# A language-model layer on one core: GpSimd's running sums move behind its scaling, its residual sum moves to the group's second sequence, and VectorE looks up the largest logits' places half an octet later

## The chip, the cores and the metric

The kernel runs on one core of one Trainium2 chip. The metric is the device time of one execution in microseconds (us); lower is better. The engines are called PE (TensorE matmul), PEld (TensorE weight load), DVE (VectorE), ACT (ScalarE), POOL (GpSimd) and SP (SyncE).

## The reference

128 sequences of 128 tokens go through an embedding, one attention layer and one mixture-of-experts layer. Cut to what matters:

```
h = concat(pos, nest, seg embeddings) @ W                    # 128 wide
h = h + attention(layernorm(h))                              # 8 heads of 64, causal softmax
x = layernorm(h)
logits = x @ router_w.T + router_b                           # 8 experts
val, idx = top_k(logits, 2); w = softmax(val)
out = h + sum_k w[k] * expert[idx[k]](x)                     # 128 -> 2*256 -> silu gate -> 128
```

## The kernel before

The kernel has two stages. The attention stage (from about 20 us to 870 us) takes the 128 sequences one after the other, and also computes, for each token, its two experts and the row that it gets in an expert-sorted table in DRAM; POOL scatters the normed tokens there with indirect DMAs. The expert stage (from about 870 us to the end) reads that table in blocks of 256 rows, and runs the experts.

In the attention stage four sequences form a group (`GB`), two groups an octet (`OB` = 8). `octet_steps` writes out by hand the order of the steps of one octet; every engine walks the same list and picks the kinds that concern it, in that order. Octets 0 and 1 are written out, octets 2 to 14 are a loop, and the last octet has an order of its own (`final_steps`, with `FINAL`). I call the stretch of one sequence a slot, number it n = 0 to 3 within its group, and call four slots a half. In each slot PE does, for the sequence k of the slot: query and key of the next group (L1209 to L1211), the scores of k (L1302, with the causal mask at L1310), then for the sequence before it, k-1, the transposes of its probabilities, first half at L1321 and second half at L1326, then one value product (L1286), the output projection (L1351) of k-2, a filler (embedding or route matmuls), and the mix (L1338) of k-1.

The probabilities come from ACT (eight exponentials with sums, L737). They are scaled by one over their sums in two halves: the first by POOL (step `scale0`, L557, which waits for DVE's reciprocals at L873 and L874), the second by DVE (step `scale1`, L946). PE's L1321 waits for the first, its L1326 for the second. scale1 of k is done in the slot after k; scale0 of k in the slot of k.

Beside this, spread over the four slots of a half:

- DVE, slot 3: `route_ranks` (copy of PE's counts, L1016), `onehot` (L883), the reciprocals, `route_logits` (L1033, L1048), `route_top` (L984 MAX8, then L990, pairs of MATCH_VALUE_LOAD and FIND_INDEX8 for each sequence, which give the places of the largest logits), `route_weight` (L1008, L1010, L1012). Slot 2: `route_choose` (L994, L997, L1003) for the group of one half earlier, reciprocals, `route_norm` (L962, L968), the low part of the transposed input (L919).
- POOL, slot 3: `route_ranks`, seven small operations that keep the running sums of rows given out per expert (L592 four times, L594, L598, L599), then `scale0`, then `residual` (L573, the bias added to h of the next group, 128x544; then L578), then two indirect DMAs of the scatter (L609). Slot 0: scale0, `rstd` (L525, L527), two DMAs. Slot 1: scale0, a small addition (L542), two DMAs. Slot 2: scale0, `route_rstd` (L533, L535), two DMAs.

The residual sum waits on a semaphore count of `scaled1`: before it can start, DVE must have scaled the last sequence of the current group, which it does at the beginning of the next slot. POOL's queue is in order, so the two DMAs behind the residual sum wait too. The first consumers of the residual are PE's and DVE's projection of the next group (L957) and the `embed_add` in slot 0 of the next half. In octet 1 POOL also has a step `w1_lo` (L561) at the end of each slot. In the last octet POOL does no scale0 (DVE does both halves, L939 and L946), and DVE's `route_apply` (L1040) waits for the scatter of two groups before.

Of the kernel before, what the change touches and what calls it, by code (L numbers as in the profile page):

```python
# [23 lines left out]
GB = 4  # L24
# [16 lines left out]
LEAD = 64  # L41
# [6 lines left out]
def octet_steps(octets_done):  # L48

    steps = []  # L50

    def late(*step):
        if step[1] + octets_done * (OB if step[0] in PER_SEQUENCE else 2) >= 0:
            steps.append(step)

    for k in range(OB):
        half, n = k // GB, k % GB
        steps.append(("query", half + 1, n))
        steps.append(("key", half + 1, n))
        steps.append(("scores", k))  # L60
        late("scale1", k - 1)
        steps.append(("max", k))
        if octets_done == 0 and k == 0:
            steps.extend(("value", 0, n) for n in range(GB))
            steps.append(("onehot", 2))
        late("probsT", k - 1)
        steps.append(("value", half + 1, n))
        late("project", k - 2)
        steps.append(("exp", k, 0))
        if n == 0:  # L70
            steps += [("embed", half + 2), ("embed_add", half + 2)]
        elif n == 1:
            steps += [("embed_r", half + 2), ("norm", half + 2)]
        elif n == 2:
            steps.append(("normT", half + 2))
            late("route_choose", half - 2)
        elif n == 3:
            late("route_ranks", half - 2)
            steps.append(("onehot", half + 3))
        steps += [("exp", k, 1), ("scale0", k)]  # L80
        late("mix", k - 1)
        if n == 0:
            steps += [("stats", half + 2), ("rstd", half + 2)]
            late("route_rows", half - 3)
        elif n == 1:
            late("route_apply", half - 2)
        elif n == 2:
            late("route_norm", half - 1)
            late("route_rstd", half - 1)
            steps.append(("xlo", half + 2))  # L90
        elif n == 3:
            late("route_logits", half - 1)
            late("route_top", half - 1)
            late("route_weight", half - 2)
            steps.append(("residual", half + 1))
        late("scatter", half - 3, 2 * n, 2 * n + 2)
        if octets_done == 0:
            steps.extend(("pad", n) for n in ((2 * k, 2 * k + 1) if k < GB else (GB + k,)))
            steps.append(("w1_hi", k))
        if octets_done == 1:  # L100
            steps.append(("w1_lo", k))
    return steps


FINAL = (
    ((("route_rows", -3), ("route_apply", -2), ("route_choose", -2)), (("scatter", -3, 0, 4),)),
    ((("route_ranks", -2), ("route_weight", -2)), (("scatter", -3, 4, 8),)),
    ((("route_rows", -2), ("route_norm", -1)), (("route_rstd", -1), ("scatter", -2, 0, 4))),
    ((("route_scale", -1), ("route_top", -1)), (("residual", 1), ("scatter", -2, 4, 8))),
    ((("route_choose", -1), ("route_ranks", -1), ("route_weight", -1)), ()),  # L110
    ((("route_rows", -1), ("route_norm", 0)), (("route_rstd", 0), ("scatter", -1, 0, 4))),
    ((("route_scale", 0), ("route_top", 0), ("route_choose", 0)), (("scatter", -1, 4, 8),)),
    ((("route_ranks", 0), ("route_weight", 0)), ()),
)


def final_steps():

    steps = []
    for k in range(OB):  # L120
        if k < GB:
            steps += [("query", 1, k), ("key", 1, k)]
        steps += [("scores", k), ("scale1", k - 1), ("max", k), ("probsT", k - 1)]
        if k < GB:
            steps.append(("value", 1, k))
        steps += [("project", k - 2), ("exp", k, 0), ("exp", k, 1), ("mix", k - 1)]
        steps += [*FINAL[k][0], ("scale0", k), *FINAL[k][1]]
    steps += [("scale1", OB - 1), ("route_rows", 0), ("scatter", 0, 0, 4)]
    steps += [("probsT", OB - 1), ("project", OB - 2), ("mix", OB - 1), ("project", OB - 1)]
    steps += [(w, 1) for w in ("route_norm", "route_rstd", "route_logits", "route_top", "route_choose", "route_ranks",  # L130
                               "route_apply", "route_weight", "route_rows")]
    return steps + [("scatter", 1, 0, 4), ("scatter", 0, 4, 8), ("scatter", 1, 4, 8)]

# [11 lines left out]
def build(nc, a, out, codes_dram, xs, spare, nseq):  # L145
# [12 lines left out]
    with ctx:  # L158
        def sb(name, shape, dt=F32):
            return ctx.enter_context(nc.sbuf_tensor(name, shape, dt))  # L160
# [78 lines left out]
        residual = [sb(f"residual{i}", [S, GB, D2]) for i in range(2)]  # L239
# [227 lines left out]
        def _(pool):  # L467
            own = [0]

            def link(ins):  # L470
                own[0] += 1
                ins.then_inc(p_own, 1)
                pool.wait_ge(p_own, own[0])
# [44 lines left out]
            def step(o, st, opening=False):  # L518
                kind, i = st[0], st[1]
                if kind == "rstd":  # L520
                    G = 2 * o + i
# [6 lines left out]
                elif kind == "route_rstd":  # L528
                    G = 2 * o + i
# [6 lines left out]
                elif kind in ("route_scale", "route_apply"):  # L536
                    G = 2 * o + i
# [25 lines left out]
                elif kind == "residual":  # L563
                    G = 2 * o + i
# [4 lines left out]

                    pool.wait_ge(h2_ready, LEAD + GB * (G - 1))  # L570
                    if not opening:
                        pool.wait_ge(scaled1, LEAD + GB * G)
                    pool.tensor_tensor(residual[i % 2][:], h[i % 2][:], bias_o[:].unsqueeze(1).broadcast_to([S, GB, D2]),  # L573
                                       ALU.add).then_inc(residual_ready, 1)
                    pool.wait_ge(rstd_ready, LEAD + G + 1)
# [3 lines left out]
                elif kind == "vsplit":  # L579
                    pool.wait_ge(tab_copied, 6)  # L580
                    link(pool.tensor_tensor(v_full_t, v_full_t, v_rest, ALU.subtract))
                    link(pool.tensor_copy(v_rest, v_full_t))
                    link(pool.tensor_scalar(v_part, v_rest, part_mask[:, 2:3], None, ALU.mult))
                    link(pool.tensor_tensor(v_full_t, v_full_t, v_part, ALU.subtract))
                    pool.tensor_copy(v_table[:], v_full_t).then_inc(s_vtable, 1)
                elif kind == "route_ranks":
                    G = 2 * o + i
                    pool.wait_ge(ranks_ready, LEAD + G + 1)
                    pool.wait_ge(filled_next, LEAD + G)
                    carry_wait(pool)  # L590
                    for j in range(GB):
                        pool.tensor_tensor(filled[:, j + 1], filled[:, j], ranks[:, 1, :, j], ALU.add).then_inc(filled_step, 1)  # L592
                        pool.wait_ge(filled_step, LEAD + GB * G + j + 1)
                    pool.tensor_tensor(rows_f[:], ranks[:, 0], filled[:, 0:GB].rearrange("p j k e -> p k j e"), ALU.add).then_inc(rows_c, 1)  # L594
                    pool.wait_ge(rows_c, LEAD + G + 1)
                    pool.wait_ge(rows_b, LEAD + G)
                    carry_wait(pool)
                    pool.tensor_tensor(rows_2[:], rows_f[:], chosen[:], ALU.mult).then_inc(rows_a, 1)  # L598
                    pool.tensor_copy(filled[:, 0], filled[:, GB]).then_inc(filled_next, 1)  # L599
                elif kind == "scatter":  # L600
                    G, par = 2 * o + i, i % 2
                    pool.wait_ge(row_ready, LEAD + G + 1)
                    pool.wait_ge(weight1_ready, LEAD + G + 1)
                    pool.wait_ge(token_ready, LEAD + G + 1)
                    pool.wait_ge(normed2_ready, LEAD + G + 1)
                    pool.wait_ge(h2_stored[par], LEAD + 16 * (o + (i - par) // 2 + 1))
                    carry_wait(pool)
                    for k, j in [divmod(n, GB) for n in range(st[2], st[3])]:
                        pool.indirect_dma_start((xs[0], xs_parts)[k], bass.IndirectOffsetOnAxis(ap=row[par][:, k, j:j + 1].bitcast(U32), axis=0),  # L609
                                                normed2[par][:, j, 0:(ROW, PART)[k]], None).then_inc(scattered[par][k], 16)  # L610
# [15 lines left out]
                for st in octet_steps(2):  # L626
                    step(o, st)
            steps = final_steps()
            n = steps.index(("route_ranks", 1)) + 1
            for st in steps[:n]:  # L630
                if st[0] != "scale0":
                    step(octets - 1, st)
# [173 lines left out]
        def _(dve):  # L806
# [69 lines left out]
            def step(o, st, opening=False, final=False):  # L876
                kind, i = st[0], st[1]
                G, b, par = 2 * o + i, OB * o + i, i % 2
# [100 lines left out]
                elif kind == "route_top":  # L979
# [3 lines left out]
                    for j in range(GB):  # L983
                        ins = V.max(top[:, j], logits[:, j])  # L984
                    ins.then_inc(top_ready, 1)
                    dve.wait_ge(top_ready, LEAD + G + 1)
                    dve.wait_ge(top_no_ready, LEAD + G)
                    carry_wait(dve)
# [487 lines left out]
```

## Time and profile before

| | |
|---|---|
| median of 3 runs | 1311.32 us (1310.25 to 1314.24) |
| the profiled execution | 1309.72 us, of which its span in the trace is 1307.9 us |
| PE busy / DVE / ACT / POOL, whole span | 92% / 81% / 73% / 66% |
| one half (four sequences) in the loop | about 24.9 us |

The span is what lies between the first and the last instruction; 1.8 us of the profiled execution lie around it. In a timeline row the columns are start (us from the span's start), duration, engine, line, operation, out<-in with shapes, count, and in brackets how long the engine was idle before it and who released it. Matmuls of one line are merged in one row, and their starts say more than their durations: where PE has no wait, the distance from one start to the next is the same in each half.

### The profile page before, as it was taken

How to read it: one execution, taken by the hardware profiler on the slowest of the kernel's cores; microseconds unless marked ns; L12 is line 12 of the kernel's file. 1: busy time of each engine (PE TensorE's matmuls, PEld its weight loads, DVE VectorE, ACT ScalarE, POOL GpSimd, SP SyncE). 2: the span in 40 equal slices, each digit the busy share in tenths (PEclk: the TensorE clock that was granted, in tenths of full speed). 3: DMA queues.
4: the chain of work that ended last, by engine and by line, in shares of the span. 5: the costliest groups of instructions: out<-in, count | busy, mean ns of one | idle time of the engine just before them, and what ended most of it. 6: DMA issues, size and time to landing. Idle time of an engine off the chain costs nothing. (4 is left out here: it accounts for less than half of the span.)

```text
span 1307.9 us, 47296 instructions
## 1 busy us (share of the span) xinstructions
PE 1196.9 (92%) x13772; PEld 1027.0 (79%) x13773; DVE 1053.9 (81%) x3980; ACT 955.4 (73%) x3352; POOL 865.8 (66%) x1207
## 2 busy tenths in 40 slices
PE   6889899999999999999999999728999997999995
PEld 4577787787877877788788787617999997899995
DVE  6568988888888888888888887747888885888885
ACT  2788899999999899989999998714555553555552
POOL 6335767767767766776776776765677774667775
PEclk8899999999999999999999999959999998999998
DMA  6141111111111111111111111238999997999994
GB/s 186 66 175 47 46 46 38 57 43 39 53 47 39 47 53 39 39 57 41 38 55 43 39 57 44 68 107 275 318 348 349 329 339 230 313 337 345 346 343 164
DMA packets 95043, 184.65 MB, mean 141 GB/s; under 512 B 18236, under 2 KB 42500, under 8 KB 94852
## 3 DMA queue, kind: packets, MB, share of 16 engines
q1 hardware_dynamic: 54404, 63.45, 15.9%
q10 hardware_dynamic: 20736, 75.80, 15.4%
q0 software_dynamic: 19840, 44.62, 9.6%
q8 instruction: 32, 0.52, 0.2%
q14 instruction: 31, 0.25, 0.1%
HBM read 46.45 MB, written 53.18 MB: 76 GB/s over the span
## 5 line engine op out<-in xcount | busy, mean ns | idle before, releaser
L737 ACT ACTIVATE probs<-ps,neg_max 128x128 f32<-128x128 f32 (+1 forms) x1024 | 336.7, 368 | 1.3 <-DVE neg_max L924 1.3
L609 POOL DMA_INDIRECT xs<-normed,row x256 | 260.8, 1019 | 70.5 <-issue 66.7
L737 ACT ACTIVATION_READ_ACCUMULATOR probs<-ps,neg_max 128x1 f32 x1024 | 240.1, 236 | 0.0
L1209 PE MATMUL ps<-xT_hi,w_now 128*128 128x256 f32 x576 | 178.8, 310 | 18.6 <-DVE xT_lo L1094 9.3
L693 ACT ACTIVATE masked<-ps,w_now 128x256 f32<-128x256 f32 x288 | 121.0, 471 | 74.2 <-PE ps L1211 69.2
L557 POOL TENSOR_TENSOR probs<-probs,inv_sums 128x384 f32<-128x384 f32 x120 | 100.1, 834 | 103.9 <-DVE inv_sums L874 103.2
L1211 PE MATMUL ps<-xT_hi,w_now 128*128 128x256 f32 x576 | 163.4, 284 | 0.0
L1210 PE MATMUL ps<-xT_lo,w_now 128*128 128x256 f32 x576 | 163.3, 284 | 0.0
L1123 DVE SCALAR_TENSOR_TENSOR probsT<-ps,w_now,masked 128x256 f32<-128x256 f32 x288 | 126.1, 479 | 43.7 <-PE ps L1211 29.9
L1391 PE MATMUL ps<-w,probsT 128*128 x1152 | 153.4, 276 | 3.0 <-DVE probsT L1123 3.0
L746 ACT ACTIVATE probsT<-ps,rstd_now 128x512 f32<-128x512 f32 x128 | 88.4, 690 | 83.7 <-PE ps L1321 75.0
L1391 PEld LDWEIGHTS ps<-w,probsT 128*128 128x128 f32 x1152 | 142.1, 193 | 3.6 <-issue 3.6
L1351 PEld LDWEIGHTS ps<-w_o,mixedT 128*128 128x128 f32 x1024 | 140.1, 193 | 6.1 <-issue 1.1
L1351 PE MATMUL ps<-w_o,mixedT 128*128 128x136 f32 x1024 | 142.1, 282 | 0.8 <-ACT mixedT L763 0.8
L1338 PE MATMUL ps<-probsT,v 128*64 128x128 f32 x2048 | 141.0, 280 | 0.0
L645 POOL DMA_INDIRECT out_h<-probs,v x108 | 104.1, 964 | 53.8 <-issue 34.5
L645 POOL DMA_INDIRECT xs<-probs,v x108 | 104.8, 970 | 51.5 <-issue 30.7
L1302 PEld LDWEIGHTS ps<-kT,qT 64*64 64x64 f32 x4096 | 97.8, 133 | 52.0 <-issue 52.0
L1209 PEld LDWEIGHTS ps<-xT_hi,w_now 128*128 128x128 f32 x576 | 110.4, 192 | 24.8 <-issue 14.5
L677 ACT CAST xT_hi<-ps 128x256 fp32r<-128x256 f32 x144 | 53.8, 373 | 93.8 <-PE ps L1371 89.9
L1302 PE MATMUL ps<-kT,qT 64*64 64x128 f32 (+1 forms) x4096 | 115.2, 250 | 5.7 <-ACT probs L737 4.3
L1338 PEld LDWEIGHTS ps<-probsT,v 128*64 128x64 f32 x2048 | 110.8, 137 | 11.9 <-issue 5.6
(236 smaller groups left out, 3090.0 us busy)
## 6 DMA issues: line engine op xcount, KB each, us to landing
w_now<-w_parts ACTq DMA_DIRECT2D x144, 514.0 KB
v<-xs SPq DMA_DIRECT2D x102, 260.0 KB
kT<-xs SPq DMA_DIRECT2D x34, 260.0 KB
xs<-pad_rows SPq DMA_DIRECT2D x16, 520.0 KB, 3.2
normed<-h SPq DMA_DIRECT2D x32, 256.0 KB, 2.6
xs<-normed,row POOLq DMA_INDIRECT x256, 2.3
w_parts<-in_w SPq DMA_DIRECT2D x1, 2048.0 KB, 9.5
xs<-probs,v POOLq DMA_INDIRECT x108
```

Source lines behind the costliest of these rows:

```text
L609: pool.indirect_dma_start((xs[0], xs_parts)[k], bass.IndirectOffsetOnAxis(ap=row[par][:, k, j:j + 1].bitcast(U32), axis=0), normed2[par][: ...
L645: pool.indirect_dma_start((xs_parts, out)[k], bass.IndirectOffsetOnAxis(ap=xt[j][:, r, GOES_TO[k]:GOES_TO[k] + 1].bitcast(U32), axis=0), y ...
L693: nc.scalar.activation(gate[z][:, f], ps[:, H1[z], f * BLK:(f + 1) * BLK], ACT.Silu, bias=b1_now[j % WBUFS][:, f:f + 1]).then_inc(gate_rea ...
L737: ins = nc.scalar.activation(probs_p[par][:, half, slots[n]], ps[:, SCORES + half, slots[n]], ACT.Exp, bias=neg_max[par][:, half, n:n + 1] ...
L1123: V.scalar_tensor_tensor(actT[z][:, f], ps[:, H2[z], f * BLK:(f + 1) * BLK], b1_now[j % WBUFS][:, 2 + f:3 + f], gate[z][:, f], ALU.add, AL ...
L1209: T.matmul(dst, w_hi_, x_hi_, start=True, stop=False)
L1210: T.matmul(dst, w_hi_, x_lo_, start=False, stop=False)
L1211: return T.matmul(dst, w_lo_, x_hi_, start=False, stop=True)
L1302: ins = T.matmul(ps[c * HQ:(c + 1) * HQ, SCORES + e, slots[n]], qT[gp][rows, pair, at + high * HQ:at + high * HQ + HQ], kT[gp][rows, pair, ...
L1338: ins = T.matmul(ps[e * HD:(e + 1) * HD, MIX, pair * S:(pair + 1) * S], v[gp][:, j, head * HD:(head + 1) * HD], probsT[:, e * PAIRS + pair ...
L1351: ins = T.matmul(ps[:, QUERY, 0:D2], mixedT[:, n], w_o[:, n], start=(n == 0), stop=(n == PAIRS - 1))
L1391: ins = T.matmul(ps[:, YB[z], r * D:(r + 1) * D], actT[z][:, half, r * S:(r + 1) * S], w2[:, bass.ds(e * 2 * D + half * D, D)], start=(hal ...
```

## The change

On POOL, the step `route_ranks` is renamed `route_fill` and stands behind `scale0` in slot 3, not before it (the PE, DVE and ACT parts of `route_ranks` stay). The `residual` step goes from slot 3, ahead of the scatter, to slot 1, behind the scatter, and its wait on `scaled1` asks for the second sequence of the current group in place of the last. On DVE the place lookup (L990) leaves `route_top` and becomes a step `route_find`, in slot 2 of the next half, ahead of `route_choose`. The last octet's lists get the same steps; there `route_find` follows `route_top` directly, but in its first slot, where it stands ahead of `route_choose`.

```diff
         elif n == 2:
             steps.append(("normT", half + 2))
+            late("route_find", half - 2)
             late("route_choose", half - 2)
         elif n == 3:
             late("route_ranks", half - 2)
             steps.append(("onehot", half + 3))
         steps += [("exp", k, 1), ("scale0", k)]
+        if n == 3:
+            late("route_fill", half - 2)
         late("mix", k - 1)
...
             late("route_logits", half - 1)
             late("route_top", half - 1)
             late("route_weight", half - 2)
+        late("scatter", half - 3, 2 * n, 2 * n + 2)
+        if n == 1:
             steps.append(("residual", half + 1))
-        late("scatter", half - 3, 2 * n, 2 * n + 2)
...
 FINAL = (
-    ((("route_rows", -3), ("route_apply", -2), ("route_choose", -2)), (("scatter", -3, 0, 4),)),
-    ((("route_ranks", -2), ("route_weight", -2)), (("scatter", -3, 4, 8),)),
+    ((("route_rows", -3), ("route_apply", -2), ("route_find", -2), ("route_choose", -2)), (("scatter", -3, 0, 4),)),
+    ((("route_ranks", -2), ("route_fill", -2), ("route_weight", -2)), (("scatter", -3, 4, 8),)),
...
                     if not opening:
-                        pool.wait_ge(scaled1, LEAD + GB * G)
+                        pool.wait_ge(scaled1, LEAD + GB * (G - 1) + 2)
                     pool.tensor_tensor(residual[i % 2][:], h[i % 2][:], bias_o[:].unsqueeze(1).broadcast_to([S, GB, D2]),
                                        ALU.add).then_inc(residual_ready, 1)
...
-                elif kind == "route_ranks":
+                elif kind == "route_fill":
                     G = 2 * o + i
                     pool.wait_ge(ranks_ready, LEAD + G + 1)
...
                     for j in range(GB):
                         ins = V.max(top[:, j], logits[:, j])
                     ins.then_inc(top_ready, 1)
+                elif kind == "route_find":
                     dve.wait_ge(top_ready, LEAD + G + 1)
```

## Rows read from the trace of the kernel before

**Rows 1.** Busy time of each engine in one stretch of the loop.

```profile
300.00:450.00 150.00, 148.58 (x1984) 119.86 (x1984) 128.91 (x543) 136.00 (x517) 104.40 (x156) 1.00 0.14 45
```

**Rows 2.** Timeline of PE: mask and transposes of three slots.

```profile
418.16 0.29 PE L1310 MATMUL ps<-causal,ident_b 64*64 64x192 bf16 x8
418.39 0.66 PE L1321 MATMUL ps<-ident,probs 128*128 128x128 f32 x4
418.88 0.60 PE L1326 MATMUL ps<-ident,probs 128*128 128x128 f32 x4
...
424.16 0.29 PE L1310 MATMUL ps<-causal,ident_b 64*64 64x192 bf16 x8
424.51 0.66 PE L1321 MATMUL ps<-ident,probs 128*128 128x128 f32 x4
425.27 0.65 PE L1326 MATMUL ps<-ident,probs 128*128 128x128 f32 x4
...
449.03 0.29 PE L1310 MATMUL ps<-causal,ident_b 64*64 64x192 bf16 x8
449.46 0.65 PE L1321 MATMUL ps<-ident,probs 128*128 128x128 f32 x4
450.16 0.66 PE L1326 MATMUL ps<-ident,probs 128*128 128x128 f32 x4
```

**Rows 3.** The same line L1321 at the loop's first and last group end.

```profile
175.41 0.66 PE L1321 MATMUL ps<-ident,probs 128*128 128x128 f32 x4
...
798.32 0.66 PE L1321 MATMUL ps<-ident,probs 128*128 128x128 f32 x4
```

**Rows 4.** Timeline of POOL in the same half.

```profile
412.77 0.98 POOL L609 DMA_INDIRECT xs<-normed,row  x1 [0.30 <-issue]
...
421.43 1.17 POOL L592 TENSOR_TENSOR filled<-filled,ranks 128x16 f32<-128x16 f32 x4 [0.29 <-DVE ranks L1016]
...
423.63 0.82 POOL L557 TENSOR_TENSOR probs<-probs,inv_sums 128x384 f32<-128x384 f32 x1
425.29 1.34 POOL L573 TENSOR_TENSOR residual<-h,bias_o 128x544 f32<-128x544 f32 x1 [0.83 <-DVE probs L946]
...
428.25 0.96 POOL L609 DMA_INDIRECT xs<-normed,row  x1 [0.30 <-issue]
```

**Rows 5.** Timeline of DVE, slot 3 and the beginning of the next.

```profile
421.77 0.13 DVE L874 RECIPROCAL inv_sums<-sums 128x2 f32<-128x2 f32 x1
...
422.03 0.19 DVE L1048 TENSOR_TENSOR logits<-raw,bias_r 128x32 f32<-128x32 f32 x1
...
422.96 0.09 DVE L990 MATCH_VALUE_LOAD top_at<-top,logits 128x8 f32 x1 [0.18 <-DVE top L984]
...
423.52 0.17 DVE L1008 TENSOR_SCALAR gap_one<-gap_exp 128x4 f32<-128x4 f32 x1
...
423.94 0.54 DVE L1012 TENSOR_TENSOR normed<-gap_exp,normed 128x4 f32<-128x4 f32 x1
...
424.65 0.56 DVE L946 TENSOR_TENSOR probs<-probs,inv_sums 128x384 f32<-128x384 f32 x1
```

**Rows 6.** Timeline of DVE, slot 2 and the beginning of slot 3.

```profile
414.81 0.15 DVE L994 TENSOR_TENSOR gap<-top 128x4 f32<-128x4 f32 x1
...
417.70 0.56 DVE L946 TENSOR_TENSOR probs<-probs,inv_sums 128x384 f32<-128x384 f32 x1
```

**Rows 7.** Timeline of DVE in the last octet: L1012 with POOL between operations.

```profile
813.12 0.17 DVE L1012 TENSOR_TENSOR normed<-gap_exp,normed 128x4 f32<-128x4 f32 x1
```

**Rows 8.** Timeline of ACT in slot 3.

```profile
419.08 0.69 ACT L746 ACTIVATE probsT<-ps,rstd_now 128x512 f32<-128x512 f32 x1 [0.35 <-PE ps L1321]
```

**Rows 9.** Timeline of PE in octet 1.

```profile
122.99 0.66 PE L1326 MATMUL ps<-ident,probs 128*128 128x128 f32 x4 [0.52 <-DVE probs L946]
...
149.64 0.65 PE L1321 MATMUL ps<-ident,probs 128*128 128x128 f32 x4 [1.58 <-POOL probs L557]
```

**Rows 10.** Timeline of DVE at the beginning of the last octet.

```profile
804.44 1.12 DVE L1040 TENSOR_SCALAR normed<-h,moments,rstd 128x128 f32<-128x128 f32 x4 [2.70 <-DMA xs<-normed,row]
```

More of the change, by code:

```diff
@@ L105 @@
 FINAL = (
-    ((("route_rows", -3), ("route_apply", -2), ("route_choose", -2)), (("scatter", -3, 0, 4),)),
-    ((("route_ranks", -2), ("route_weight", -2)), (("scatter", -3, 4, 8),)),
+    ((("route_rows", -3), ("route_apply", -2), ("route_find", -2), ("route_choose", -2)), (("scatter", -3, 0, 4),)),
+    ((("route_ranks", -2), ("route_fill", -2), ("route_weight", -2)), (("scatter", -3, 4, 8),)),
     ((("route_rows", -2), ("route_norm", -1)), (("route_rstd", -1), ("scatter", -2, 0, 4))),
-    ((("route_scale", -1), ("route_top", -1)), (("residual", 1), ("scatter", -2, 4, 8))),
-    ((("route_choose", -1), ("route_ranks", -1), ("route_weight", -1)), ()),
+    ((("route_scale", -1), ("route_top", -1), ("route_find", -1)), (("residual", 1), ("scatter", -2, 4, 8))),
+    ((("route_choose", -1), ("route_ranks", -1), ("route_fill", -1), ("route_weight", -1)), ()),
     ((("route_rows", -1), ("route_norm", 0)), (("route_rstd", 0), ("scatter", -1, 0, 4))),
-    ((("route_scale", 0), ("route_top", 0), ("route_choose", 0)), (("scatter", -1, 4, 8),)),
-    ((("route_ranks", 0), ("route_weight", 0)), ()),
+    ((("route_scale", 0), ("route_top", 0), ("route_find", 0), ("route_choose", 0)), (("scatter", -1, 4, 8),)),
+    ((("route_ranks", 0), ("route_fill", 0), ("route_weight", 0)), ()),
 )
@@ L129, in final_steps @@
     steps += [("probsT", OB - 1), ("project", OB - 2), ("mix", OB - 1), ("project", OB - 1)]
-    steps += [(w, 1) for w in ("route_norm", "route_rstd", "route_logits", "route_top", "route_choose", "route_ranks",
+    steps += [(w, 1) for w in ("route_norm", "route_rstd", "route_logits", "route_top", "route_find", "route_choose", "route_ranks", "route_fill",
                                "route_apply", "route_weight", "route_rows")]
@@ L628, in _ @@
             steps = final_steps()
-            n = steps.index(("route_ranks", 1)) + 1
+            n = steps.index(("route_fill", 1)) + 1
             for st in steps[:n]:
```

## The prediction

> **What bounds the kernel now.** I read the busy table by windows first. In the loop of the attention stage PE is busy 148.6 of 150 us [rows 1], the others clearly less, at the full granted clock. So PE sets the pace, and an edit that touches only DVE and POOL can gain no more than what PE loses by waiting. The expert stage is untouched by the diff, and I cost it at nothing.
>
> Then I read PE's timeline, and compared the same lines in different slots. In slot 3, where nothing is late, L1321 starts 0.23 us behind the mask, and L1326 0.49 behind L1321. In slot 0, behind the group's last sequence, the two distances are 0.35 and 0.76 in one half, and 0.43 and 0.70 in the other [rows 2]. PE loses 0.12 + 0.27 = 0.39 us in the first and 0.20 + 0.21 = 0.41 in the second, 0.40 on the mean, once per half. The busy table hides a part of this, since the loss sits between matmuls that are shown as long. From the first of these places in the steady part to the last one are 622.9 us [rows 3]; they stand 24.92 us apart, so there are 26. The whole pool is 26 x 0.40 = 10.4 us in the loop.
>
> Last I read the two engines that PE waits for there. POOL's scale0 runs from 423.63 to 424.45 and L1321 follows at 424.51; but its reciprocals were done at 421.90, and POOL spent 421.43 to 423.63 on the running sums in between [rows 4, 5]. DVE's scale1 ends at 425.21 and L1326 follows 0.06 later; DVE came to it late because of what it does ahead of it, the lookup of 0.56 us (422.96 to 423.52) with 0.18 us of semaphore wait, and L1012, which takes 0.54 us for four columns [rows 5]. The same L1012 takes 0.17 where POOL runs nothing beside it [rows 7]: in slot 3 it starts at 423.94, inside scale0, and ends at 424.48, just when POOL lets go. All of that lies in the step that the change rebuilds.
>
> **Part 1, running sums behind scale0.** The seven operations keep their cost of 2.2 us [rows 4]. scale0 can start 0.2 us after the reciprocals, about 422.1, and end at 422.9, while PE wants it at 424.3: the 0.12 and 0.20 go, with 1.4 us to spare. The sums then run to about 425.1 and the scatter's two DMAs to about 427.7 where they ended at 429.21 before [rows 4]: 1.5 us earlier. The consumer of the sums is DVE's row step, late in slot 0, behind the embedding and its statistics. Cost: nothing, hidden under PE.
>
> The price is what scale0 now meets on DVE. L1012 is free of it (0.37 us won). But the logits sum L1048, at 422.03, has two SBUF inputs as L1012 has, and is issued within 0.1 us of the new scale0. From below it costs nothing (DVE is first). From above it is held to the end of scale0, 0.73 us [rows 5].
>
> **Part 2, the lookup leaves slot 3.** DVE gains 0.56 + 0.18 there. With the 0.37 that is 1.11 us, so scale1 ends at 424.10, or at 424.83 if the logits are held. L1326 at its undisturbed distances would start at 424.16 + 0.23 + 0.49 = 424.88, and needs scale1 done 0.06 before, at 424.82 [rows 2, 5]. In both cases the 0.27 and 0.21 go, in the worse one with nothing to spare. I take the free case, because DVE issues first.
>
> By the Trainium skill (SBUF — State Buffer, "Who interferes with whom") a VectorE instruction with two SBUF inputs contends with a GpSimd instruction that reads SBUF, and whoever is first makes the other block fully; L1012's 0.54 against 0.17 agrees. By that rule alone the change moves a block from L1012 to L1048 if POOL gets there first, and the sum is then 10.4 less some hundredths per half; if DVE gets there first, it is the 10.4.
>
> **Part 3, the lookup enters slot 2.** It stands ahead of L994 (414.81) and pushes all that DVE does behind it by 0.56 us, up to scale1 of this slot's sequence at the beginning of slot 3, which ends at 418.26 and would end at 418.82. PE wants it at 418.88 - 0.06 = 418.82 [rows 2, 6]. The slack is used up to the hundredth. I charge 0.02 us per half, 0.5 in all; if the lookup is slower there, each further tenth costs PE 2.6 us. This is the tightest place of the change. The same sequence's L1321, at 418.39, waits on POOL's scale0 of 0.82 us. The pushed reciprocals stand a few small operations behind L994, and would have to come later than about 417.3 to be felt.
>
> **Part 4, the residual sum.** Its 1.34 us come behind the scatter of slot 1, which ends at 413.75 [rows 4]. Its wait for the second sequence's scale1 is met by then (that multiply runs a slot, some 6.2 us, before the one at 417.70), so it runs from 413.8 to 415.2. The first consumer is more than a half away, nothing is late behind it. Beside it DVE does the value sum and the projection (each with one input from PSUM), then the lookup (one input each), then, at 415.37, L994 with two SBUF inputs, 0.2 us after the residual's end. Cost zero, bounded above in the rival below. It frees the scatter of slot 3 from the wait of 0.83 us and the sum itself.
>
> **Ahead of the loop and behind it.** In octet 1 PE waits for the same two things at the ends of both halves, 1.58 us and 0.52 [rows 9]; 2.1 us are there to be won. POOL has its weight split in that octet too, which now lands elsewhere beside DVE. Bounds 0 and 2.1; I take 1.8. At the start of the last octet DVE waits 2.70 us for the landing of the scatter [rows 10], whose DMAs now end 1.5 us earlier. The lookup is put behind that wait and takes 0.56 back, and part of it is the slot's own gain, counted already. Bounds 0 and 1.5; I take 0.8. The residual in the last octet runs late in POOL's queue already, so the new wait changes nothing there.
>
> **Sum.** 10.4 - 0.5 + 1.8 + 0.8 = 12.5 us. The profiled execution took 1309.72 (1.8 around its span), which would become 1297.2; it lies 1.6 below the median of the runs, 1311.32, which would become 1298.8. Its own range is 1294 to 1302.5: without octet 1 and the last octet 9.9, with both at their upper bounds and no charge in slot 2 14.0, and one to three microseconds for what follows a late transposition, which I did not count.
>
> **Rivals.**
>
> *Half of it.* scale0 is out of the way, but scale1 of the last sequence stays late, because the logits are held and then L1012 and the multiply itself meet the running sums (their operations are 0.2 to 0.3 us each, and L1012 and L946 have two SBUF inputs). For it: the held case leaves no slack. Against: the same sums ran beside L1048 before, which took 0.19. Then only 26 x 0.16 = 4.2 is won, less 0.5, plus about 1.8 outside: 5.5, and 1305.8.
>
> *Slower: L994 runs into the residual sum.* If the residual starts late enough to be under way when L994 and the lookup are due, DVE stands still until its end, up to 0.75 us for an end at 416.1. Behind slot 2's used-up slack PE pays all of it: 26 x 0.75 = 19.5 against 10.4, and nothing outside the loop, so about 1320. It decides from 0.40 us per half (no gain) and is slower by over 0.3% from 0.55. For it: L1012 shows that such a block is whole. Against: by the scatter's end the residual is over 0.2 us before L994. A mild form, 0.3 to 0.5 us, lies within 0.3%.
>
> *PE's wait is replaced.* ACT's shortest idle time ahead of PE's transposes is 0.35 us [rows 8], less than the 0.40 that a half loses; if ACT became the bound, little would be won, about 1308. Against: it is idle in each of the four slots, starts from PE's transposes each time, and so moves with them. The change is then worth 3 us.
>
> **How the numbers follow.** The forecast has 64 in 100, half of it 16, the replaced wait 6, the residual's block 14, of which 8 severe. A measurement of this kernel can tell about 0.3%, 3.9 us, from no change. Faster: 64, 10 of the half case and 2 of the replaced wait, 76. Slower: the 8 severe. The remaining 16 are within. The range reaches from 1293 to 1307, which takes in the forecast and the half case, 80 in 100.
>
> **What the profile after would show.** Right: L557 of slot 3 ahead of L592 and ending more than a microsecond before L1321; L1321 0.23 behind the mask and L1326 0.49 behind L1321 in slot 0; L1012 at 0.17; halves 24.5 us apart; L573 directly behind a scatter in slot 1; DVE's wait at the start of the last octet near 1.2. Wrong: an L1326 in slot 3 later than 0.49 behind L1321, an L994 or L990 longer than 0.16 in slot 2, L1048 near 0.9, or a wait on L557 in slot 2.

## The result

The changed kernel takes 1303.73 us (median of 9 runs, 1298.32 to 1307.82) where the kernel before takes 1310.25 us (median of 9, 1307.41 to 1314.24). The ratio is 0.9944, with a 95% interval of 0.9920 to 0.9968: faster, by 3 to 8 per mille. The forecast was 12.5 us less than before, 0.95%; the measured gain is 6.5 us by the medians and 7.3 us by the ratio. The sign and the range held, the size is a little over half of what was forecast.

The profiled execution of the changed kernel took 1301.83 us, its span is 1299.7 us. First the busy table by windows, one stretch of the loop; the columns are busy time and instructions of PE, PEld, DVE, ACT and POOL, then the granted clock, the DMA share and GB/s. It answers to [rows 1]:

```profile
300.00:450.00 150.00, 149.68 (x2034) 121.62 (x2028) 128.52 (x558) 138.37 (x527) 107.52 (x160) 1.00 0.14 46
```

PE is busy 1.1 us more of each 150 and does more work in it (the count of its matmuls went up from 1984 to 2034). The timeline of PE (all lines of this kernel's PE code stand five further down: mask L1315, transposes L1326 and L1331) in one slot 3 and the slot 0 behind it, which answers to [rows 2]:

```profile
757.09 0.29 PE L1315 MATMUL ps<-causal,ident_b 64*64 64x192 bf16 x8
757.31 0.66 PE L1326 MATMUL ps<-ident,probs 128*128 128x128 f32 x4
757.97 0.66 PE L1331 MATMUL ps<-ident,probs 128*128 128x128 f32 x4
...
763.29 0.29 PE L1315 MATMUL ps<-causal,ident_b 64*64 64x192 bf16 x8
763.52 0.66 PE L1326 MATMUL ps<-ident,probs 128*128 128x128 f32 x4
764.01 0.60 PE L1331 MATMUL ps<-ident,probs 128*128 128x128 f32 x4
```

In slot 0 the distances are 0.23 and 0.49 now, as if nothing were late: both waits are gone. In slot 3 the second distance is 0.66 in the first half of each octet (as here) and 0.49 in the second; the 0.66 is one of the prediction's own signs of being wrong. The group ends that answer to [rows 3]:

```profile
174.05 0.66 PE L1326 MATMUL ps<-ident,probs 128*128 128x128 f32 x4
...
787.93 0.66 PE L1326 MATMUL ps<-ident,probs 128*128 128x128 f32 x4
```

25 halves lie between them, 24.56 us each, against 24.92: 0.36 us less per half, 9.0 us in the 25. The 26 of the prediction count the group ends themselves, of which there is one more. POOL's timeline in one half, the counterpart of [rows 4]: the residual sum directly behind the scatter of slot 1, then in slot 3 scale0 (L561) ahead of the running sums (L596), and the last scatter:

```profile
384.12 1.35 POOL L577 TENSOR_TENSOR residual<-h,bias_o 128x544 f32<-128x544 f32 x1
...
392.53 0.83 POOL L561 TENSOR_TENSOR probs<-probs,inv_sums 128x384 f32<-128x384 f32 x1 [0.63 <-DVE inv_sums L878]
393.32 1.11 POOL L596 TENSOR_TENSOR filled<-filled,ranks 128x16 f32<-128x16 f32 x4
...
397.62 0.97 POOL L613 DMA_INDIRECT xs<-normed,row  x1 [0.30 <-issue]
```

And DVE's in the same half, the counterpart of [rows 6] and [rows 5]: L999 is the difference of the two largest logits behind the lookup, L1053 the logits, L1017 the small product that was held before, L950 scale1.

```profile
385.55 0.14 DVE L999 TENSOR_TENSOR gap<-top 128x4 f32<-128x4 f32 x1
...
388.48 0.56 DVE L950 TENSOR_TENSOR probs<-probs,inv_sums 128x384 f32<-128x384 f32 x1
...
392.47 0.19 DVE L1053 TENSOR_TENSOR logits<-raw,bias_r 128x32 f32<-128x32 f32 x1
...
393.63 0.22 DVE L1017 TENSOR_TENSOR normed<-gap_exp,normed 128x4 f32<-128x4 f32 x1
394.10 0.18 DVE L877 RECIPROCAL inv_sums<-sums 128x4 f32<-128x4 f32 x1 [0.25 <-issue]
...
394.36 0.56 DVE L950 TENSOR_TENSOR probs<-probs,inv_sums 128x384 f32<-128x384 f32 x1
```

L1017 takes 0.22 us and not 0.54. The logits L1053 are issued 0.06 us before scale0 and are not held. scale0 ends at 393.36, 1.46 us before PE's transposes at 394.82. This is a half that ends a turn of the loop, and behind L1017 DVE issues nothing for 0.25 us.

Where the gain ends can be read from one row of PE, its first transposes of the expert stage. Before:

```profile
882.38 0.66 PE L1371 MATMUL ps<-ident,v 128*128 128x128 f32 x2 [16.00 <-DMA v<-xs]
```

After:

```profile
870.53 0.66 PE L1376 MATMUL ps<-ident,v 128*128 128x128 f32 x2 [15.90 <-DMA v<-xs]
```

The attention stage is 11.85 us shorter in this pair. From there to the end of the span it is 425.5 us before and 429.2 after: the expert stage, whose code is the same, takes 3.7 us more in this pair.

### The profile page after: what moved, and what is told of

It is laid out like the page before. It is cut to its first block and busy times, and to the rows that moved or that the text cites. A ratio compares the mean times of both kernels' runs of the same rounds, so it can differ in the third digit from the quotient of the medians.

```text
span 1299.7 us, 47309 instructions
## 1 busy us (share of the span) xinstructions
PE 1193.7 (92%) x13772; PEld 1028.0 (79%) x13773; DVE 1043.3 (80%) x3980; ACT 953.5 (73%) x3352; POOL 870.2 (67%) x1207
## 5 line engine op out<-in xcount | busy, mean ns | idle before, releaser
L561 POOL TENSOR_TENSOR probs<-probs,inv_sums 128x384 f32<-128x384 f32 x120 | 99.6, 830 | 98.4 <-DVE inv_sums L878 97.6
L649 POOL DMA_INDIRECT out_h<-probs,v x108 | 104.2, 964 | 55.7 <-issue 29.3
```

Of the source, the lines that this page charges most:

```text
L649: pool.indirect_dma_start((xs_parts, out)[k], bass.IndirectOffsetOnAxis(ap=xt[j][:, r, GOES_TO[k]:GOES_TO[k] + 1].bitcast(U32), axis=0), y ...
```

## Experiments

Where an experiment gave one run, I use mainly what its trace shows of the loop, since that repeats from octet to octet within a few hundredths. What is said "in the loop" is the difference between its first and its last group end, 25 halves apart. I call the halves of an octet the first and the second; the slot 0 behind the second one's end lies behind the turn of the loop. Each edit is shown against the changed kernel, and the cut of the expert stage is the same in both kernels.

**The attention stage alone.** Both kernels end when the table of blocks is made and the scatters have landed. The expert stage is left out, and the output is not computed.

```diff
-            for k in range(TOPK):
-                with pool.Fori(k * (PH // XBUFS), (k + 1) * (PH // XBUFS)) as i:
+            for k in range(0):
```
(and the like on the other engines)

> The kernel before without its expert stage (all engines stop when the table of blocks is made and the scatters have landed; the output is not computed). The trace of before ends this stage at about 885 us, so about 890 us with the end of a program. It is the base for the next run. If the missing part of the forecast lies in the expert stage, the runs of this kernel agree within 1 us or so.

> The changed kernel without its expert stage (output not computed). My theory: the attention stage alone wins what the traces show, 11 to 12 us against the run before it (9.4 in the loop, the rest ahead of it and at its end), in every round; the full kernel shows less only because its expert stage takes some us more or less from run to run. Rival: the two full traces are a lucky pair, and the attention stage wins about 7 us, as the median of the full runs has it.

Measured: 890.51 us (887.89 to 892.62, 4 runs) and 881.21 us (880.29 to 882.79, 4 runs), 9.3 us less. The two sets don't overlap, so the attention stage gains, clear of the expert stage. The 9.3 is between the two expectations, 11 to 12 and 7, and four runs each don't decide between them: the sets are 5.1 us apart at their nearest and 12.3 at their farthest. The runs spread more than the 1 us I expected, 4.7 and 2.5 us, so the attention stage has a variation of its own (below). The pair of traces of the full kernels, 11.85, was above the medians' difference.

**Running sums alone.** Only `route_fill` behind scale0.

```diff
-            late("route_find", half - 2)
...
             late("route_top", half - 1)
+            late("route_find", half - 1)
...
-        if n == 1:
+        if n == 3:
             steps.append(("residual", half + 1))
```
(the residual ahead of the scatter again, with its wait of before)

> Only the running sums move behind scale0; the lookup and the residual sum stay in slot 3. Theory (L1012 was held by scale0): both distances in slot 0 are undisturbed or nearly, since scale1 ends 0.37 us earlier, 424.84 against 424.82 wanted; halves of 24.52 us, 10 us less in the loop. Rival (the lookup is what made scale1 late): only the distance to the first transposes goes, the second stays at 0.70 to 0.76; halves of 24.76, 4.2 us less.

Measured: halves of 24.77 us, 0.15 less than before, 3.6 us in the loop. The distance to the first transposes is 0.22 in all slots, as expected. The second is 0.53 at the end of the first half and 0.99 at the end of the second. DVE and PE in the latter, at the end of the loop's body:

```profile
345.31 0.17 DVE L1017 TENSOR_TENSOR normed<-gap_exp,normed 128x4 f32<-128x4 f32 x1
345.78 0.18 DVE L877 RECIPROCAL inv_sums<-sums 128x4 f32<-128x4 f32 x1 [0.30 <-issue]
```
```profile
346.71 0.66 PE L1331 MATMUL ps<-ident,probs 128*128 128x128 f32 x4 [0.33 <-DVE probs L950]
```

L1017 is free (0.17), as my theory had it, and in the first half that gives all but 0.04. In the second half scale1 is late in spite of it: DVE issues nothing for 0.30 us ahead of the first instruction of the next turn of the loop. That gap was not in my working. In the kernel before, the held product covers the same stretch:

```profile
349.22 0.54 DVE L1012 TENSOR_TENSOR normed<-gap_exp,normed 128x4 f32<-128x4 f32 x1
```

Its next reciprocals start at 349.69, 0.47 us behind it, and here 0.47 us behind L1017 too (345.31 and 345.78). So in the half that ends a turn, freeing this product gives DVE nothing. Neither expectation holds as written: the theory is right in one half, and in the other even a little is lost.

**Lookup alone.** Only `route_find` in slot 2.

```diff
-        if n == 3:
-            late("route_fill", half - 2)
...
             late("route_ranks", half - 2)
+            late("route_fill", half - 2)
```
(and the residual as in the kernel before)

> Only the lookup moves to slot 2; running sums ahead of scale0, residual sum in slot 3. Theory: scale0 still ends at PE's first transposes or later, because scale1 now comes early and meets it at GpSimd's port: what the second transposes win the first lose, and slot 2 pays 0.1 us; halves of 24.9 to 25.1 us, 0 to 5 us more than before in the loop. Rival (the lookup alone was the cause of scale1's lateness): the second distance goes to 0.49, the first stays, halves of 24.7, 6 us less.

Measured: halves of 25.02 us, 0.10 more than before, 2.5 us in the loop: the theory. DVE, POOL and PE of the slot 0 behind the first half, one row or two of each timeline:

```profile
325.04 0.66 DVE L949 TENSOR_TENSOR probs<-probs,inv_sums 128x384 f32<-128x384 f32 x1
```
```profile
325.22 0.52 POOL L602 COPY filled<-filled 128x16 f32<-128x16 f32 x1
325.72 0.82 POOL L560 TENSOR_TENSOR probs<-probs,inv_sums 128x384 f32<-128x384 f32 x1
```
```profile
326.59 0.66 PE L1325 MATMUL ps<-ident,probs 128*128 128x128 f32 x4 [0.60 <-POOL probs L560]
```

scale1 is early and starts while POOL is still at the last of its running sums. POOL's copy of 16 columns, 0.2 us otherwise, takes 0.52 and ends 0.04 behind scale1 (325.74 and 325.70). scale0 comes behind it and PE's first transposes are 0.89 behind the mask. Here DVE holds POOL. Behind the second half scale0 is the first, by 0.19 us, and POOL holds DVE, whose multiply takes 1.05 us in place of 0.56:

```profile
350.31 0.82 POOL L560 TENSOR_TENSOR probs<-probs,inv_sums 128x384 f32<-128x384 f32 x1
```
```profile
350.50 1.05 DVE L949 TENSOR_TENSOR probs<-probs,inv_sums 128x384 f32<-128x384 f32 x1
```

**Residual sum alone, and the change without the running sums' move.** These two, and the first runs of the next two kernels, landed on another chip, where the kernel before takes 1488.81 us.

```diff
-        if n == 3:
-            late("route_fill", half - 2)
```
(`route_fill` back ahead of scale0; for the residual alone the lookup back in slot 3 too)

> Only the residual sum moves to slot 1 (with its wait); running sums ahead of scale0, lookup in slot 3. Theory: PE's distances in slot 0 stay as before (0.35 and 0.76, 0.43 and 0.70), halves of 24.92 us; only the scatter of slot 3 is earlier, and DVE's wait at the start of the last octet shrinks from 2.70 us to about 1.2: 0 to 1.5 us less in all. Rival (the residual in slot 1 costs something): an L994 or a multiply in slots 1 and 2 is held, and halves grow.

> The change without the move of the running sums. Theory: as the lookup alone, halves of 24.9 to 25.1 us: without the sums out of scale0's way the other two parts win nothing in the loop. Rival: the parts add up, and this one has half of the gain, 24.7.

Measured: 1501.65 and 1500.29 us, halves of 27.1 and 26.7 us. They can't be compared with 24.92. In each half PE's transposes of slot 3 come some 8.1 us behind those of slot 2 there, where before they come 6.3 us behind. The trace has waits at that place for which it names no releaser of this core; a row of the waits of the first of them, from 300 to 700 us, seven and a half octets (total us, times, longest):

```profile
DVE neg_max L926 <- remote: 30.6, 15, 2.1
```

What can still be read is a slot away from that place. With the residual alone the distances in slot 0 of the first half are those of before:

```profile
230.71 0.29 PE L1314 MATMUL ps<-causal,ident_b 64*64 64x192 bf16 x8
231.06 0.66 PE L1325 MATMUL ps<-ident,probs 128*128 128x128 f32 x4
231.82 0.44 PE L1330 MATMUL ps<-ident,probs 128*128 128x128 f32 x2
```

0.35 and 0.76: at this place the residual sum was in no one's way. Behind the second half the distances are 1.07 and 0.68, and 0.43 and 0.70 before, so that half can't be read. Without the running sums' move the first of the two places shows 0.73 and 0.49, like the lookup alone (0.89 and 0.49). Whether the halves would be 24.9 to 25.1 us is not shown, since neither ran on a chip with the regular loop.

**The change without the residual sum's move.**

```diff
-        late("scatter", half - 3, 2 * n, 2 * n + 2)
-        if n == 1:
+        if n == 3:
             steps.append(("residual", half + 1))
+        late("scatter", half - 3, 2 * n, 2 * n + 2)
```
(and its wait on `scaled1` as before)

> The change without the move of the residual sum: running sums behind scale0, lookup in slot 2. Theory: the loop is that of the change, halves of 24.56 us, since the residual sum was in nobody's way there; it gives its part outside the loop, in octet 1 and at the start of the last octet, 1 to 2 us. Rival: in slot 3 the residual sum and its wait hold GpSimd, or DVE's next operations, and halves are 24.6 to 24.8.

Measured: 1302.40 us, one run; halves of 24.59 us against the change's 24.56, 0.03 more: the theory, nearly, and just below the rival's 24.6. PE's first expert transposes are at 870.20, where the change has 870.53, but octet 0 ran 3.4 us shorter here (its eighth transposes start at 92.70, the change's at 96.05). From those to the attention stage's last transposes it is 747.51 us here (to 840.21) and 745.99 in the change (to 842.04). The change is 1.5 us shorter there: 0.8 in the loop, 0.45 between octet 0 and the first group end, and 0.3 behind the last. So the residual sum's move gives 0.7 us outside the loop in this pair of traces, less than the 1 to 2 expected.

**The lookup twice in slot 2.** The first pass writes a tile that nobody reads.

```diff
+                    for j in range(GB):
+                        V.max_index(top_at_x[:, j], top[:, j], logits[:, j])
                     for j in range(GB):
                         ins = V.max_index(top_at[:, j], top[:, j], logits[:, j])
```

> The changed kernel with the lookup done twice in slot 2 (the second result is not used): 0.56 us more for DVE there. Theory: slot 2 has no slack left, so PE pays all of it in slot 3, L1326 (of the old numbering) 0.5 to 0.7 us later than 0.49: halves of 25.1 us, 14 us more than the change. Rival: slack elsewhere takes it up, under 5 us more.

On the other chip: 1504.48 us, halves of 26.6, not comparable. The same kernel again:

> The same kernel as before under this name, the lookup done twice in slot 2 (second result not used), on a chip whose loop is regular. Theory: no slack is left in slot 2, so halves are 24.56 + 0.5 = 25.1 us, 13 to 15 us more than the change. Rival: DVE has slack elsewhere in the half that takes it up, halves under 24.75.

Measured: 1321.32 us, halves of 24.96, 0.41 more than the change, 10.2 us in the loop. PE in slot 3 of the first half:

```profile
769.30 0.66 PE L1329 MATMUL ps<-ident,probs 128*128 128x128 f32 x4
770.38 0.66 PE L1334 MATMUL ps<-ident,probs 128*128 128x128 f32 x4 [0.42 <-DVE probs L951]
```

1.08 against 0.66 in the change, and 0.82 against 0.49 in the other half. PE pays 0.42 of the extra 0.56 us in the one, 0.33 in the other. So the change has used up slot 2's slack in the first half, where it was late already, and a quarter of a microsecond is left in the second. Where the other 0.14 of the first half went is not shown. The theory, with no slack in both, was too strict.

**The residual sum twice in slot 1.** The first result is not used.

```diff
+                    pool.tensor_tensor(residual_x[:], h[i % 2][:], bias_o[:].unsqueeze(1).broadcast_to([S, GB, D2]), ALU.add)
                     pool.tensor_tensor(residual[i % 2][:], h[i % 2][:], bias_o[:].unsqueeze(1).broadcast_to([S, GB, D2]),
                                        ALU.add).then_inc(residual_ready, 1)
```

> The changed kernel with the residual sum done twice in slot 1 (the first result is not used): GpSimd is busy 1.3 us longer, over the time when the difference of the two largest logits is due on DVE. Theory (whole block): DVE's difference, 0.15 us in the change, takes 1.2 to 1.4 us, and PE pays 1.0 to 1.2 us in slot 3, some 28 us in the loop. The lookup ahead of it (one SBUF input each) keeps its 0.07 and 0.16. Rival: GpSimd and DVE share the port, both a little slower, under 8 us.

On the other chip: 1487.02 us. Its difference L1001 took 1.37 us in one half there, ending with POOL's second sum, and 0.14 or 0.15 in twelve others; PE's price is not to be read from it. The same kernel again:

> The same kernel as before under this name, the residual sum done twice in slot 1 (first result not used). Theory: the difference of the two largest logits on DVE is held until GpSimd's end, 1.4 us in place of 0.15, and PE pays it in slot 3: halves of 25.6 to 25.8 us, 27 to 32 us more than the change. The lookup ahead of it is not held. Rival: under 8 us.

Measured: 1328.58 us, halves of 25.33, 0.78 more than the change, 19.5 us in the loop. POOL's second sum, and DVE beside it:

```profile
344.30 1.34 POOL L579 TENSOR_TENSOR residual<-h,bias_o 128x544 f32<-128x544 f32 x1
```
```profile
344.26 0.16 DVE L997 FIND_INDEX8 top_at<-top,logits 128x8 uint32<-128x8 f32 x1
344.34 1.34 DVE L1001 TENSOR_TENSOR gap<-top 128x4 f32<-128x4 f32 x1
```

The difference of four columns takes 1.34 us and ends 0.04 us behind POOL's sum. The lookup ahead of it ran beside the first sum in its usual 0.07 and 0.16. In the first half the difference takes 0.95 us. The mechanism of the slower rival is real, and whole. PE's second distance in slot 3 is 1.29 in the first half and 1.30 to 1.35 in the second, so it pays 0.6 of the 0.8 that DVE loses in the one and 0.8 of 1.2 in the other, less than I wrote.

**The change with a split lookup and an earlier weight split.**

```diff
             late("route_top", half - 1)
+            late("route_find", half - 1, 0, 2)
...
-            late("route_find", half - 2)
+            late("route_find", half - 2, 2, GB)
...
             steps.append(("w1_hi", k))
-        if octets_done == 1:
-            steps.append(("w1_lo", k))
+            if k >= GB:
+                steps.append(("w1_lo", k - GB))
+        if octets_done == 1 and k < GB:
+            steps.append(("w1_lo", k + GB))
```

> The changed kernel with two more edits. The lookup is split: two of its four sequences stay in slot 3, where DVE waits 0.25 us for nothing it computes and PE has 0.3 us to spare, and two go to slot 2. GpSimd's weight split w1_lo moves from the slots of octet 1 to slots 4 to 7 of octet 0 and 0 to 3 of octet 1, away from the scatter. Theory: the 0.17 us in every second slot 3 goes (halves of 24.46 us, 2.7 us less in the loop than the change), and of the 4.2 us that PE still waits in the second half of octet 1 about 3 go: first expert transposes at 865 us, 5 to 6 us before those of the change, and 1.2% faster than the kernel before, within what the expert stage adds from run to run. Rival: the split lookup makes slot 3 late instead (0.1 to 0.3 us in slot 0), and the weight split meets the padding of octet 0; nothing beyond the change.

Measured: 1296.29 us (1295.03 to 1301.34, 6 runs), before beside it 1311.34 (11 runs), ratio 0.9886, interval 0.9851 to 0.9921. It is the fastest of all, 1.1% below the kernel before where 1.2% was expected; against the change, which did not run beside it, the intervals touch. Its first expert transposes:

```profile
867.48 0.66 PE L1381 MATMUL ps<-ident,v 128*128 128x128 f32 x2 [18.09 <-DMA v<-xs]
```

3.05 us earlier than the change's, less than the 5 to 6 expected. The attention stage's last transposes are 6.5 us earlier (835.56 and 842.04); the stretch between the two took 31.92 us here and 28.49 in the change. In the loop nothing is won, halves are 24.55. The 0.17 us of slot 3 are gone (first pair), and slot 0 at the end of the loop's body, where DVE's 0.30 us without issue lies, is late by 0.14 instead (second pair):

```profile
752.18 0.66 PE L1331 MATMUL ps<-ident,probs 128*128 128x128 f32 x4
752.67 0.60 PE L1336 MATMUL ps<-ident,probs 128*128 128x128 f32 x4
...
733.53 0.66 PE L1331 MATMUL ps<-ident,probs 128*128 128x128 f32 x4
734.16 0.66 PE L1336 MATMUL ps<-ident,probs 128*128 128x128 f32 x4
```

For the lookup's part the rival was right in the loop. The gain lies in octet 1: from the eighth transposes to the first group end it is 73.0 us where the change has 78.0, and in the second half of octet 1 the second distances are 0.49, 0.49 and 0.59, where the change has 1.33, 1.62 and 1.22. I put it down to the weight split; both edits are in this kernel, and no run has the one without the other.

## Why the prediction was right, and where its size was off

**The bound and the pool.** PE's waits in slot 0 were what DVE and POOL could give back, 0.40 us per half. Both distances went to their undisturbed value. This step held.

**Part 1 and part 2.** scale0 ends 1.46 us before it is wanted (1.4 forecast), L1012 is freed, the logits are not held, scale1 is in time. Of the 1.11 us that DVE was to gain, 1.07 are there behind the first half: against PE's mask scale1 goes from 0.49 us behind it to 0.58 ahead. Behind the second half it goes from 0.52 behind to 0.24 ahead, 0.76: the gap of the loop's turn takes back the 0.37 of L1012, which the prediction counted in both. scale1 is in time all the same. What the parts alone show is that they don't add: the running sums alone win 0.15 us per half, the lookup alone loses 0.10, and both together win 0.33 (the change without the residual). The working put both on one chain, and that was right. It did not say that the lookup without the running sums would cost time; the expectation of its run did.

**Part 3.** The tightest place was named rightly, and its price was too low: 0.02 us per half was charged, and slot 3 pays 0.17 in every second half, and the value product behind it 0.05 more, 0.11 per half. The half that pays is the one from which the slack was read. The slack of 0.56 us was right; what was wrong is that DVE would be pushed by the lookup's 0.56 and no more. DVE in slot 2 and at the beginning of slot 3, in the half of the first transposes at 757.31:

```profile
753.64 0.30 DVE L961 TENSOR_TENSOR h<-ps,residual 128x136 f32<-128x136 f32 x1 [0.53 <-PE ps L1356]
...
757.35 0.56 DVE L950 TENSOR_TENSOR probs<-probs,inv_sums 128x384 f32<-128x384 f32 x1
```

scale1 starts 0.04 us behind PE's first transposes, where it stood 0.69 ahead of them (417.70 and 418.39 [rows 2, 6]): it is pushed by 0.73, and 0.73 less 0.56 is the 0.17. Of that, 0.12 were there ahead of the lookup: L961 starts 3.67 us ahead of the transposes and stood 3.80 ahead before (414.59), because its wait for PE's projection grew from 0.41 to 0.53. Why PE's result comes later to it is not shown. In the second half DVE stood waiting for ACT before, which takes up a part of the push:

```profile
789.16 0.18 DVE L873 RECIPROCAL inv_sums<-sums 128x4 f32<-128x4 f32 x1 [0.23 <-ACT probs L737]
```

There scale1 is pushed by 0.34 only, and PE pays nothing. The two halves of an octet are not alike, and the slack of one was taken for both.

**Loop in sum.** Forecast 9.9 us, shown 9.0 between the first and the last group end, and 26 x 0.36 = 9.4 with the last one itself.

**Part 4.** The residual sum costs nothing in slot 1 of the loop, as forecast: in the half shown it ends 0.08 us before L999 starts (385.47 and 385.55), closer than the 0.2 us I had, and in the other 0.38 before. Its move is worth 0.03 us per half and 0.7 us outside the loop, by one pair of traces. In octet 1 the rival's block did happen once, in slot 6:

```profile
137.15 1.58 DVE L999 TENSOR_TENSOR gap<-top 128x4 f32<-128x4 f32 x1
```
```profile
141.97 0.66 PE L1331 MATMUL ps<-ident,probs 128*128 128x128 f32 x4 [0.97 <-DVE probs L950]
```

Residual sum and weight split now lie back to back on POOL (135.98 to 138.70), and L999 is held till their end. PE loses 1.1 us that it didn't lose before. Without the residual sum's move this distance is 0.49, so the block is the move's.

**Outside the loop.** These are the terms of the sum that were mis-sized most in the attention stage. From the beginning to the group end at 175.41 the forecast was 1.8 us; it was 1.36, of which 0.68 were there before octet 1 begins, where nothing was forecast, so octet 1 gave 0.7. The new block took 1.1 of it, and in the first turn of the loop slot 3 is 0.41 us late. At the last octet 0.8 was forecast. DVE's wait there:

```profile
793.14 1.12 DVE L1045 TENSOR_SCALAR normed<-h,moments,rstd 128x128 f32<-128x128 f32 x4 [2.12 <-DMA xs<-normed,row]
```

2.12 and not the 1.2 that I named as its mark [rows 10]. The last scatter starts 1.50 us behind the group end and not 2.40 as before, 0.9 earlier in the slot where I had 1.5, and the lookup behind the wait takes 0.56 back. DVE also comes to the wait 0.3 us sooner, so its length was a poor mark. PE's next transposes are 8.37 us behind those of the group end where they were 8.54: 0.17 won, and the group end itself, counted with the loop, has 0.27 of its own. So nothing was left of the 0.8. Another 1.35 us are won between the attention stage's last transposes and the first of the expert stage (29.84 us before, 28.49 after), which I had not forecast. The six other traces with a regular loop have 29.3 to 31.9 us there, so this can be chance.

**Down to the measured 6.5.** The attention stage alone gives 9.3 us. Its own variation comes from octet 0 at least: the eighth transposes start at 96.7 us before, at 96.1 after, and between 92.7 and 98.5 in the other traces from chips with a regular loop. The rest is the expert stage, costed at nothing. In the eight full traces of such chips it takes between 424.1 and 432.0 us from PE's first transposes there to the end of the span: 425.5 before, 429.2 after, and 424.1 with the running sums alone, 429.4 with the lookup alone, where its code is the same too. So a pair of runs can differ by 8 us through it. The two shortest of the eight are those of the two kernels that keep the lookup whole in slot 3; with one trace of each kernel that can be chance. The interval of the full kernels' ratio, 4 to 10 us, holds the 9.3. Whether the change makes the expert stage a little longer, or the medians of nine runs fell so, stays open: with this variation it would take many more runs, and none was made for it.

**The rivals.** The half case did not occur in the change; its 0.16 us per half is near to the 0.15 that the running sums alone give, though for another reason, the turn of the loop. ACT did not become the bound: it is busy 138.4 of 150 us and PE 149.7. The severe block did not occur in the loop, and was made on purpose by the doubled sum.

## What to carry to other kernels

When one engine is nearly full, compare the distances between the same instructions in different turns; a place where they are longer is a wait, even where the busy table shows none. Read the slack of each parity of an unrolled loop by itself, and look at the turn's end too. And before an operation with two SBUF inputs is put on VectorE, or a long one on GpSimd, look at what the other does at that time: a product of four columns can cost a whole scaling.

## What the runs showed of the hardware

VectorE and GpSimd hold each other whole in these traces, in both directions, and only with some instructions. On VectorE the sums and products with two SBUF inputs were held: 1.34 us in place of 0.15 beside GpSimd's sum, 0.54 in place of 0.17 beside its scaling. MATCH_VALUE_LOAD and FIND_INDEX8 kept their 0.07 and 0.16 us beside the same sum. GpSimd's copy of 16 columns took 0.52 in place of 0.2 beside VectorE's scaling. The Trainium skill (SBUF — State Buffer, "Who interferes with whom") says that VectorE's instructions with two SBUF inputs contend, that those with at most one don't unless they run in a mode that uses both port pairs, and that the first to be issued wins; the traces agree, down to a lead of 0.06 us for the logits. One input alone is no safe sign: the four operations of `route_apply`, which scale and shift a tile of 128x128 each, take 1.69 to 1.73 us in all where GpSimd's scaling runs beside them, before and after alike, and 1.11 where it doesn't. Whether they run in such a mode no run shows.

At the end of each turn of the loop DVE issues nothing for 0.24 to 0.30 us, in the traces where it is not late for another reason (0.30 in the one with the running sums alone, 0.24 to 0.25 in the change). I took it for part of the loop's branch because of its place, which no run tested.

A chip on which the kernel before takes 1488.81 us, 13 to 14% more than on the others, showed the same durations of instructions where nothing holds them, some 1.8 us more between slots 2 and 3 of each half, with waits that have no releaser of this core, and a slower expert stage (244 to 255 GB/s in most slices of the profile where the kernel before has 313 to 349 on its own chip). The cause is open.
